# Pixel sums as f32 in buffers of their own, one f32 product in place of three f16 ones, a third of the sums on GpSimd, tap powers stored column by column

## The reference

```
xp = x.reshape(B, C, nH, P, nW, P).transpose(0, 1, 2, 4, 3, 5).reshape(B, C, N, P, P)
xf = jnp.fft.rfft2(xp, norm='ortho').real
xf = xf * freq_weight_h[:, None] * freq_weight_w[None, :]
x_proj = xf.transpose(0, 2, 1, 3, 4).reshape(B, N, C * P * PW) @ proj_w.T + proj_b
out = jnp.concatenate([cls, x_proj], axis=1) + position_embeddings
...
K = jnp.einsum('dn,dnl->dl', coef, vand)      # taps: powers exp(dA * l), summed over n
h = h + ssm_conv(layernorm(h), K)
h = h + moe(layernorm(h))
```

## Time and profile before

| | us |
|---|---|
| median of 3 runs | 1430.72 (1425.78 to 1434.66) |
| profiled execution | 1433.11 |
| its span, first to last instruction | 1431.3 |
| `embed`, from the start to the first load of `mix` | 253.7 |
| PE busy, share of the span | 76% |
| DVE busy | 68% |
| ACT busy | 38% |
| POOL busy | 47% |

### The profile page before, as it was taken

How to read it: one execution, slowest core, us unless ns; L and a number is a source line. 1 busy time by engine, 2 the same in 40 slices (tenths; PEclk the granted TensorE clock), 3 DMA queues, 4 the chain that set the end, 5 groups by cost and what they waited for, 6 DMA issues and landing times. The chain is left out here.

```text
span 1431.3 us, 27592 instructions
## 1 busy us (share of the span) xinstructions
PE 1090.5 (76%) x8823; PEld 742.9 (52%) x8824; DVE 972.6 (68%) x2944; ACT 545.2 (38%) x992; POOL 673.2 (47%) x712
## 2 busy tenths in 40 slices
PE   2868998745188989898989898985799999999000
PEld 2656776635045555555545555553466666666000
DVE  7998887211376867686757676776588888888255
ACT  1134565311243333333333333342355555555000
POOL 2356786000045453545353635362277777777200
PEclk9867999778589999999999999998899999999555
DMA  6446785897952322232321323125344444443499
GB/s 238 166 167 213 256 260 143 225 230 135 236 145 71 70 65 68 68 70 64 68 66 49 84 55 78 49 64 182 89 129 126 129 126 132 132 133 114 135 370 339
DMA packets 213258, 198.10 MB, mean 138 GB/s; under 512 B 69712, under 2 KB 192114, under 8 KB 212910
## 3 DMA queue, kind: packets, MB, share of 16 engines
q1 hardware_dynamic: 166904, 131.86, 33.2%
q0 software_dynamic: 19488, 39.17, 7.9%
q10 hardware_dynamic: 26774, 25.89, 6.7%
HBM read 123.58 MB, written 74.41 MB: 138 GB/s over the span
## 5 line engine op out<-in xcount | busy, mean ns | idle before, releaser
L1548 POOL DMA_INDIRECT parts<-unit_yu,unit_token x208 | 225.4, 1084 | 73.7 <-issue 73.7
L1128 POOL DMA_INDIRECT routed<-rows_w,slot x198 | 210.1, 1061 | 55.3 <-issue 55.3
L1297 DVE SCALAR_TENSOR_TENSOR hf<-psu,sg 128x512 f32<-128x512 f32 (+1 forms) x150 | 101.7, 678 | 160.6 <-PE psu L978 160.1
L1059 ACT ACTIVATE sg<-psg 128x512 f32<-128x512 f32 (+1 forms) x150 | 89.0, 593 | 227.7 <-PE psg L978 227.5
L978 PE MATMUL psg<-xt,ffn_w_hi 128*128 128x512 f16 (+1 forms) x450 | 154.6, 399 | 0.0
L992 PE MATMUL pso<-ffn_w_hi,hh 128*128 128x192 f16 x594 | 146.3, 246 | 2.8 <-DVE hl L1304 1.6
L978 PE MATMUL psu<-xt,ffn_w_hi 128*128 128x512 f16 (+1 forms) x450 | 148.2, 384 | 0.0
L992 PE MATMUL pso<-ffn_w_hi,hl 128*128 128x192 f16 x594 | 146.1, 246 | 0.0
L992 PE MATMUL pso<-ffn_w_lo,hh 128*128 128x192 f16 x594 | 146.1, 246 | 0.0
L414 PE MATMUL ps<-w_hi,xh 128*98 128x192 f16 x384 | 109.2, 284 | 41.3 <-POOL xl L336 41.3
L1111 POOL TENSOR_TENSOR ve<-mv,eps 128x4 f32<-128x4 f32 (+1 forms) x25 | 4.9, 195 | 279.7 <-DVE mv L1171 279.7
(11 more groups left out here) (219 smaller groups left out, 2902.4 us busy)
## 6 DMA issues: line engine op xcount, KB each, us to landing
unit_xu<-routed SPq DMA_DIRECT2D x53, 392.0 KB
area<-in_xa_dram SPq DMA_DIRECT2D x48, 392.0 KB, 4.7
area<-in_xb_dram SPq DMA_DIRECT2D x48, 392.0 KB, 5.8
part<-parts SPq DMA_DIRECT2D x48, 384.0 KB, 9.3
toeplitz<-taps SPq DMA_DIRECT2D x24, 600.2 KB
resid<-h ACTq DMA_DIRECT2D x32, 294.0 KB
hin<-resid SPq DMA_DIRECT2D x24, 384.0 KB, 3.7
yin<-mixed SPq DMA_DIRECT2D x96, 96.0 KB, 3.8
```

What stands on the lines that cost most here:

```text
L1059: nc.scalar.activation(sg[m % 2][:, 0:n], psg[:, m % 2, 0:n], ACT.Silu, scale=1.0 / SCALE).then_inc(s["sg_ready"], 1)
L1128: nc.gpsimd.indirect_dma_start(out=routed[:, :], out_offset=bass.IndirectOffsetOnAxis(ap=slot[q][:, k, t:t + 1], axis=0), in_=rows_w[q][:, ...
L1297: ins = nc.vector.scalar_tensor_tensor(out=hf[i][:, 0:n], in0=psu[:, i, 0:n], scalar=1.0 / SCALE, in1=sg[i][:, 0:n], op0=ALU.mult, op1=ALU ...
L1548: nc.gpsimd.indirect_dma_start(out=parts[:, :], out_offset=bass.IndirectOffsetOnAxis(ap=token[q][:, k:k + 1], axis=0), in_=y[q][:, k, :], ...
```

## The change

- The sums get buffers of their own, `xf` (f32, two sets of three colours); `area` is only read. `xh`, `xl`, `w_hi`, `w_lo` are gone; `w` is the weight in f32, `w_xh` the f16 part that `w_x` needs.
- DVE adds colours 0 and 1, POOL colour 2. Both wait ahead of `fold(g)` until PE has done with group g-2 (`tokens_ready`), whose buffer is written again. ACT's `split` and POOL's `low` are gone.
- PE: one f32 product for each colour in place of three f16 ones.
- A slot of `area` is free for the next load when its sum is done (`folded0`, `folded1`, `folded2`).
- `zq` is stored as `[DH, KB]`, the 14 powers of a channel together, in reverse, as `zp` is. PE then reads its moving operand without steps; DVE's instructions that write and read `zq` step by 14 elements.

```diff
-        zq, = pieces_of(free[1], ((2, KB, DH),))
+        zqd, = pieces_of(free[1], ((2, DH, KB),))
+        zq = zqd.rearrange("p k d b -> p k b d")[:, :, ::-1]
...
-        xh = [sb(f"xh{i}", [ROWS, C, GT], F16) for i in range(2)]
-        xl = [sb(f"xl{i}", [ROWS, C, GT], F16) for i in range(2)]
+        xf = [sb(f"xf{i}", [ROWS, C, GT]) for i in range(2)]
...
-                        sp.wait_ge(s["xl_ready"], n - NSLOT + 1)
+                        sp.wait_ge(s[f"folded{c}"], g - NSLOT // C + 1)
...
-            nc.scalar.copy(w_hi[:].rearrange("p (i c) e -> p i (c e)", i=2), psw).then_inc(s["whi_ready"], 1)
+            nc.scalar.copy(w_xh[:], psw[:, 1, D:2 * D])
+            nc.scalar.copy(w[:, 0:2].rearrange("p c e -> p (c e)"), psw[:, 0])
+            nc.scalar.copy(w[:, 2], psw[:, 1, 0:D]).then_inc(s["whi_ready"], 1)
...
-            def low(g):
-                for c in range(C):
-                    n = C * g + c
-                    pool.wait_ge(s["xh_ready"], n + 1)
-                    nc.gpsimd.tensor_tensor(xl[g % 2][:, c], xa[n % NSLOT][:], xh[g % 2][:, c],
-                                            ALU.subtract).then_inc(s["xl_ready"], 1)
+            def fold(g):
+                n = C * g + C - 1
+                pool.wait_ge(x_in[n % NSLOT], 32 * (n // NSLOT + 1))
+                if g >= 2:
+                    pool.wait_ge(s["tokens_ready"], GI * (g - 1))
+                nc.gpsimd.tensor_tensor(xf[g % 2][:, C - 1], xa[n % NSLOT][:], xb[n % NSLOT][:],
+                                        ALU.add).then_inc(s["folded2"], 1)
...
-                                            zq[part, k, ::-1, ch].rearrange("n b d -> n d b"),
+                                            zqd[part, k, ch].rearrange("n d b -> n (d b)"),
...
-                pe.wait_ge(s["xl_ready"], C * g + C)
+                for c in range(C):
+                    pe.wait_ge(s[f"folded{c}"], g + 1)
...
-                            nc.tensor.matmul(out, xh[i][:, c, t], w_hi[:, c], start=(c == 0), stop=False)
-                            nc.tensor.matmul(out, xh[i][:, c, t], w_lo[:, c], start=False, stop=False)
-                            nc.tensor.matmul(out, xl[i][:, c, t], w_hi[:, c], start=False, stop=False)
+                            nc.tensor.matmul(out, xf[i][:, c, t], w[:, c], start=(c == 0), stop=False)
...
             def fold(g):
-                for c in range(C):
+                if g >= 2:
+                    dve.wait_ge(s["tokens_ready"], GI * (g - 1))
+                for c in range(C - 1):
                     n = C * g + c
                     dve.wait_ge(x_in[n % NSLOT], 32 * (n // NSLOT + 1))
-                    nc.vector.tensor_tensor(xa[n % NSLOT][:], xa[n % NSLOT][:], xb[n % NSLOT][:],
-                                            ALU.add).then_inc(s["folded"], 1)
+                    nc.vector.tensor_tensor(xf[g % 2][:, c], xa[n % NSLOT][:], xb[n % NSLOT][:],
+                                            ALU.add).then_inc(s[f"folded{c}"], 1)
...
-            nc.vector.tensor_tensor(w_lo[:, 0:2].rearrange("p c e -> p (c e)"), psw[:, 0],
-                                    w_hi[:, 0:2].rearrange("p c e -> p (c e)"), ALU.subtract)
-            nc.vector.tensor_tensor(w_lo[:, 2], psw[:, 1, 0:D], w_hi[:, 2], ALU.subtract)
```

More of the change, by code:

```diff
@@ L165, in embed @@
         fx, = pieces_of(free[2], ((2, C, ROWS),))
-        w_hi = sb("w_hi", [ROWS, C + 1, D], F16)
-        w_lo = sb("w_lo", [ROWS, C, D], F16)
+        w = sb("w", [ROWS, C, D])
+        w_xh = sb("w_xh", [ROWS, D], F16)
         w_x = sb("w_x", [ROWS, D], F16)
@@ L207, in embed @@
                  "kf_ready", "zero_ready", "taps_out", "k0_in", "yc_ready", "out_done",
-                 "add_ready", "folded", "xh_ready", "xl_ready", "eh_ready", "es_ready", "tokens_ready",
+                 "add_ready", "folded0", "folded1", "folded2", "eh_ready", "es_ready", "tokens_ready",
                  "h_ready", "stats_ready", "mv_ready", "ve_ready", "rs_ready", "mr_ready", "nb_ready", "const_ready",
@@ L278, in _ @@
             act.dma_start(pos[:], io["pos"][1]).then_inc(s["pos_in"], 16)
-            def split(g):
-                for c in range(C):
-                    n = C * g + c
[L283 to L286, removed]
             def rest_high(m):
@@ L318, in _ @@
                     rest_high(step // QG)
-                if step < NG:
-                    split(step)
                 if 0 <= step - 2 < NG:
@@ L369, in _ @@
                 if step < NG:
-                    low(step)
+                    fold(step)
         @block.tensor
@@ L593, in _ @@
             dve.wait_ge(s["whi_ready"], 1)
-            nc.vector.tensor_tensor(w_lo[:, 0:2].rearrange("p c e -> p (c e)"), psw[:, 0],
-                                    w_hi[:, 0:2].rearrange("p c e -> p (c e)"), ALU.subtract)
-            nc.vector.tensor_tensor(w_lo[:, 2], psw[:, 1, 0:D], w_hi[:, 2], ALU.subtract)
-            nc.vector.scalar_tensor_tensor(out=w_x[:], in0=w_hi[:, C], scalar=signs[:, 0:1], in1=psw[:, 1, D:2 * D],
+            nc.vector.scalar_tensor_tensor(out=w_x[:], in0=w_xh[:], scalar=signs[:, 0:1], in1=psw[:, 1, D:2 * D],
                                            op0=ALU.mult, op1=ALU.add).then_inc(s["w_ready"], 1)
```

## The result

The changed kernel takes 1442.03 us (median of 20 runs, 1435.0 to 1449.31), the kernel before 1432.37 us (20 runs). The ratio is 1.006, with a 95% interval from 1.0045 to 1.0076: 0.6% slower, and the whole interval lies above 1. Forecast was 0.3% faster, 1427 us, with 1444 as the upper end. The profiled execution took 1440.37 us.

What follows compares the result with a forecast made beforehand. PE was taken to bound embed from group 5 on, DVE to set group 5's start; -10.8 us there and +6.7 on PE's groups gave -4.1, 1429.0 for the profiled execution, so 1427 us; range 1414 to 1444.

Steps and rivals of the forecast that it cites:

- if PE does not idle ahead of group 5, the 5.2 us come back: PE's groups 5 to 15: the 5.2 us lost to the lower clock level before would be regained.
- group 4 would begin at the lower level, take 17.3 us and arrive when DVE does: PE's group 4: first 13.3 us at the lower level, 17.3 us in all, reaching group 5 with the clock up.
- the rival with chance 0.14: The clock falls again ahead of group 5 because PE waits for DVE: +6.5 us, 1433; chance 0.14.
- T1: When PE's group 5 can start, set by DVE's work up to fold(5): 109.9 instead of 120.7, -10.8 us.
- DVE's wait for the weights: POOL's first two sums fall into the 2.70 us DVE waits anyway; up to 1 us if they lasted longer.
- The f32 instruction: PE's blocks: an f32 instruction of 192 columns takes 0.163 us, between 0.160 and 0.177, at the upper clock level.
- 0.345 us go to the 18-row product and the change of rows around it, which stays: PE's blocks: this share of the 1.083 us stays the same with f32, making a block 1.32 us.
- The tap pair: A pair of tap products on PE falls from 0.937 to about 0.555 us without the step of 96: -9.2 us.
- the wide f32 weight load sets PE's pace: Rival: f32 weight loads, not the step, slow PE's products: +9.2 and +14.3, together 1450; chance 0.12.
- The cost of the strided `zq` on DVE: DVE's chain(2), ahead of group 5: 5184 elements handled with steps, +3.3 us, with the start-up +3.5.
- the slack of DVE, POOL and the loads in groups 6 to 15: DVE needs at most 8.4 us a group against PE's 10.6, hidden; POOL has slack; slots are loaded two groups ahead.
- four terms of 5 to 21 us (-10.8, +21.1, -9.2 and -5.2): Group 5's earlier start -10.8, f32 blocks on PE +21.1, tap pairs -9.2, clock loss regained 5.2 us.

Runs made afterwards that it cites:

- keep_clock: Changed kernel plus 15 extra f32 products of the weight with itself in group 4, ahead of the last image's products, result overwritten; ratio to before 1.0043.
- sum3_dve: Changed kernel with all three sums of a group on DVE and none on POOL; ratio to before 1.0024.
- es_sum3: Changed kernel with the 18-row products of an image's two halves side by side and all sums on DVE; ratio to before 0.9923.
- es_pair: Changed kernel with the 18-row products of an image's two halves side by side, same products and sums; ratio to before 0.9993.
- both runs on the taps: Kernel before with only the tap powers stored column by column, ratio 0.9955; changed kernel with tap powers stored as before, ratio to before 1.0075.
- spread: Changed kernel with the tap powers' chain cut into seven pieces instead of five and tap products in groups 7 to 12; ratio to before 1.0007.

## Why the prediction was wrong

It had PE's end 4.1 us earlier, and it came 9.05 us later. The 13 us between are four terms, in the order of their size.

1. **The clock at group 5 (5.0 us).** The step that failed is "if PE does not idle ahead of group 5, the 5.2 us come back", and the reason given for it, that group 4 would begin at the lower level, take 17.3 us and arrive when DVE does. Group 4 began at 96.1, was at the lower level for 3.6 us only, and was done at 108.6; DVE's `chain(4)` and `fold(5)` let PE wait for 5.15 us. The 17.3 us rested on the 13.3 us at the lower level that the f16 kernel had shown once. The clock fell, as the rival with chance 0.14 had it, for 10.2 us. From 113.85 to the end are 138.8 us, and 88 x 1.357 + 24 x 0.598 is 133.8. `keep_clock` shows the cause: filled, 4.3 us come back.

2. **T1, group 5's start (4.0 us).** 113.85 came in place of 109.9. The mechanism was right (DVE's stalls, then the chain), sizes were off. The second of POOL's sums did not fall into DVE's wait for the weights but 2.7 us behind its end, since its pixels landed later (22.12): 1.6 us. The four others stalled DVE by 1.5 to 1.7 us each instead of 1.45: 0.6. DVE's work on the weights began 1.4 us later, and behind a load that landed later (first instruction at 8.74 instead of 7.32), and its wait for ACT's copies ended 1.56 us later (19.47 instead of 17.91). ACT's three copies so took 0.14 us more than the one, less than the 0.3 allowed, and 1.2 us of this term are the late landing, which is likely the execution's own: the same instruction starts at 8.72 in `keep_clock`, 8.03 in `sum3_dve` and 7.06 in `es_sum3`. The rest, 0.5, is spread. `sum3_dve` confirms the stalls: without POOL's sums, and with the landing taken off, group 5 starts 2.6 us earlier although DVE does six sums more.

3. **The block (3.0 us).** The f32 instruction was sized right: six take 1.15 us from the first to the 18-row product (105.92 to 107.07), with 0.1625 us between starts. But "0.345 us go to the 18-row product and the change of rows around it, which stays" failed by 0.034: it is 0.38 us with f32. `es_pair` shows that the 0.38 us belong to the change of rows. The trace shows where the 0.034 are: behind the 18-row product the first two f32 instructions start 0.242 us apart instead of 0.163, 0.08 more, and the first two f16 products 0.121 apart instead of 0.082, 0.04 more. That a weight load, longer for f32, stands in the open there is argued.

4. **The tap pair (1.0 us).** 0.598 instead of 0.555 us; the step of 96 elements was the reason, as both runs on the taps show.

The rival "the wide f32 weight load sets PE's pace" was wrong: with a load of 98 columns between each two, f32 instructions start 0.1625 us apart, and with loads of 120 columns the later tap instructions 0.105 us apart. The cost of the strided `zq` on DVE, 3.5 us, and the slack of DVE, POOL and the loads in groups 6 to 15 were right: between 200 and 240 PE is idle for 0.58 of 40 us, nearly all of it ahead of group 12 (209.29), where it waits for ACT's `kf` of the tap products and for no sum.

The range held the measured median, but the sign was wrong: four terms of 5 to 21 us (-10.8, +21.1, -9.2 and -5.2) nearly cancelled in the sum, and the rivals on the slower side were priced each by itself, while here one of them came nearly whole and two terms missed by 3 and 4 us beside it. The balance as measured: the f32 products cost 88 x (1.357 - 1.083) = 24.1 us in the stretch that is PE's, the taps give back 8.1 there, and group 5 starts 6.9 us earlier; the clock costs what it cost before. That leaves the 9 us. Of the 6.9 us, 1.9 are DVE's (`fold(5)` at 111.27 instead of 113.13: the 10 us of stalls that ended were for the most part spent again on POOL's sums and on `zq`), and 5.0 come from the halves, which no longer lie between `fold(5)` and PE (2.6 us instead of 7.6).

## What to carry to other kernels

Before a step is taken off one engine and put on another, find the stretch in which each of them ends the waits: here ACT and POOL, which had slack in all later groups, were relieved at the cost of PE, which had none. A wait that disappears ahead of a bound engine is worth its length only if that engine arrives then; otherwise it becomes idle time, and for PE idle time can be paid a second time in clock (5 us here). Where a short product on few rows stands between wide ones, try such products side by side: in the changed kernel this gave about 9 us, 0.29 us for each pair, but only 0.13 where products on yet other rows stand between the wide ones.

## What the runs showed of the hardware

- Idle times of PE of 5.15 us (ahead of 113.85) and 4.58 us were followed by 10 to 17 us at the lower clock level; one of 0.97 us was not. The length of the idle time alone does not tell how much follows: 2.86 us (`spread`) and 3.42 us (`sum3_dve`) were followed by 14 and 9 us of work at the lower level, 5.65 us (`es_pair`) and 5.29 us (`es_sum3`) by 4; and the level fell after 1.66 us in the kernel before (ahead of 50.36), but not after 1.60 us in `es_pair` (ahead of 202.80). Why is open. Useless products in the gap were worth 4.3 us in one kernel and 6.6 us of `embed` in another.
- A PE that is hardly ever idle is no guarantee of the upper level: with one f32 call and one 18-row product a block, PE stayed at the lower level through eleven groups (a block of 1.21 us) in which it was idle for 1.74 us in all. This was one execution.
- After the long idle time at the start, f32 products reached the upper level 8.6 us after the first of them (29.65 to 38.3 us), the f16 ones of before 15.1 us after theirs (33.36 to 48.46). Those fell back to the lower level from 51.9 to 58.7, after PE had been idle for 1.66 us (ahead of 50.36).
- An f32 call of 192 columns (0.325 us, two instructions) costs as much as four f16 products of the same columns (0.082 us each), so that one in place of three is a loss of 0.08 us a call, not counting the change of rows.
- A change between 128 and 18 rows of the array and back costs 0.34 us among f16 products and 0.38 us among f32 ones, the 18-row product included; a second 18-row product beside the first adds 0.12 us.
